# Moving TensorE's broadcast of B behind the y sums and products of its step

## The reference, cut to what matters

```python
dA = jnp.exp(jnp.einsum('ble,en->blen', delta, A))
dBu = jnp.einsum('ble,bln,ble->blen', delta, Bm, u)
def step(h, inp):
    dA_t, dBu_t, C_t = inp
    h = dA_t * h + dBu_t
    y_t = jnp.einsum('ben,bn->be', h, C_t)
    return (h, y_t)
```

## Time and profile before

| | |
|---|---|
| median of 3 runs | 494.55 us (493.66 to 495.66) |
| the profiled execution's own time | 495.33 us |
| its span | 493.5 us |
| busy: PE / DVE / ACT / POOL | 406.7 / 447.3 / 378.1 / 422.7 us |
| idle of PE just before the broadcast | 37.7 us |
| idle of DVE just before `dbu` | 3.7 us |
| mean granted clock of PE | 0.94 |

### The profile page before, as it was taken

How to read it: one execution, slowest core, us unless ns; L and a number is a source line. 1 busy time by engine, 2 the same in 40 slices (tenths; PEclk the granted TensorE clock), 3 DMA queues, 4 the chain that set the end, 5 groups by cost and what they waited for, 6 DMA issues and landing times. The chain is left out here.

```text
span 493.5 us, 6708 instructions
## 1 busy us (share of the span) xinstructions
PE 406.7 (82%) x2133; PEld 279.7 (57%) x2164; DVE 447.3 (91%) x539; ACT 378.1 (77%) x690; POOL 422.7 (86%) x236
## 2 busy tenths in 40 slices
PE   7969665997499698997799788996899697687796
PEld 3537444675358456674558556664658455565474
DVE  6698899979999899989999889988999889999852
ACT  4478975598867898698967898698966898687715
POOL 6159899999999789998999899988999789999810
PEclk9999987997889989998999999998999989599799
DMA  6673045200830028300742027300741027300001
GB/s 168 160 298 151 1 144 222 87 0 1 301 126 27 0 42 327 108 0 2 248 149 77 2 66 303 106 2 0 259 156 60 1 62 306 107 2 21 0 1 43
DMA packets 24146, 51.06 MB, mean 103 GB/s; under 512 B 4521, under 2 KB 14256, under 8 KB 20016
## 3 DMA queue, kind: packets, MB, share of 16 engines
q1 hardware_dynamic: 24112, 50.64, 30.1%
HBM read 48.01 MB, written 2.62 MB: 103 GB/s over the span
## 5 line engine op out<-in xcount | busy, mean ns | idle before, releaser
L606 POOL TENSOR_TENSOR hc<-h,c_rows 128x1024 f32<-128x1024 f32 x127 | 298.4, 2366 | 27.0 <-DVE h L1382 26.3
L1382 DVE TENSOR_TENSOR_SCAN h<-dA,state,dbu 128x512 f32<-128x512 f32 x192 | 234.2, 1266 | 13.2 <-ACT dA L697 13.2
L697 ACT ACTIVATE dA<-delta,a_neg 128x512 f32<-128x512 f32 x256 | 173.2, 685 | 45.3 <-DVE h L1382 44.9
L1123 PE MATMUL yb<-ident,hc 128*128 128x128 f32 x1024 | 155.1, 287 | 17.8 <-POOL hc L606 16.6
L1123 PEld LDWEIGHTS yb<-ident,hc 128*128 128x128 f32 x1024 | 131.0, 149 | 64.9 <-issue 45.0
L1395 DVE TENSOR_TENSOR dbu<-du,bb 128x1024 f32<-128x1024 f32 x88 | 105.5, 1199 | 3.7 <-PE bb L1148 2.0
L593 POOL TENSOR_TENSOR dbu<-du,b_rows 128x1024 f32<-128x1024 f32 x40 | 94.6, 2364 | 4.1 <-DMA b_rows<-bc_dram 4.1
L1382 DVE TENSOR_TENSOR_SCAN h<-dA,dbu 128x512 f32<-128x512 f32 x64 | 74.2, 1205 | 5.5 <-ACT dA L697 5.4
L1023 PE MATMUL mf<-f_hT,w_conv 128*128 128x512 f32 x112 | 54.6, 612 | 2.0 <-ACT zu L757 1.4
L1148 PE MATMUL bb<-b_parts,sel 128*128 128x512 bf16 x63 | 25.1, 399 | 37.7 <-DVE dbu L1395 36.4
L1148 PEld LDWEIGHTS bb<-b_parts,sel 128*128 128x128 bf16 x88 | 8.6, 98 | 56.5 <-DVE dbu L1395 36.9
(11 more groups left out here) (206 smaller groups left out, 524.2 us busy)
## 6 DMA issues: line engine op xcount, KB each, us to landing
c_rows<-bc_dram SPq DMA_DIRECT2D x32, 1024.0 KB, 7.5
b_rows<-bc_dram SPq DMA_DIRECT2D x40, 256.0 KB, 8.9
xs<-in_L_attn_x_dram SPq DMA_DIRECT2D x8, 256.0 KB, 3.6
out_dram<-xs SPq DMA_DIRECT2D x7, 256.0 KB, 5.6
ygT<-in_L_attn_conv_w_dram SPq DMA_DIRECT2D x2, 256.0 KB, 4.3
bc_dram<-xd SPq DMA_DIRECT2D x8, 64.0 KB, 1.6
w_in<-in_L_attn_W_in_dram SPq DMA_DIRECT2D x2, 128.0 KB, 4.2
probT<-in_L_wmod_dram SPq DMA_DIRECT2D x1, 256.0 KB, 4.2
```

The lines of the kernel that those rows point to most:

```text
L606: nc.gpsimd.tensor_tensor(hc[:, pair % RC, :, :], h[:, pair % RH, :, :], c_rows[:, q, n % NQ, :].unsqueeze(1).broadcast_to([P, HALVES, T]) ...
L697: nc.scalar.activation(dA[ke % RD][:, :], delta[:, ge % 2, half, :], ACT.Exp, scale=a_neg[:, half, n:n + 1]).then_inc(s_dA, 1)
L1123: last = nc.tensor.matmul(bank[:, tile], hc[:, pair % RC, half, tile], ident[:, :], start=False, stop=n == N - 1, is_transpose=True, skip_ ...
L1382: v.tensor_tensor_scan(h[:, pair % RH, half, :], dA[k % RD][:, :], dbu[:, pair % RW, half, :], start, ALU.mult, ALU.add).then_inc(s_scan, 1)
```

## The change

The block that makes the broadcast moves from the head of PE's step to behind the y sum, the products of both sides and the correction product of B. Its condition, its waits and its instruction stay as they are, and no other engine's list changes.

```diff
                 for s in range(STEPS):
                     k = g * STEPS + s
                     kf, ks = k + AHEAD_FILL, k - LAG_SUM
-                    if 0 <= kf < K and kf % HALVES == 0 and kf // HALVES % N not in POOL_N:
-                        pair = kf // HALVES
...
-                        nc.tensor.matmul(bb[mine % RB][:, :], sel[:, n, :], b_parts[:, gf % 2, :],
-                                         start=True, stop=True).then_inc(s_fill, 1)
                     if 0 <= ks < K:
                         y_sum(ks)
                     for side in JOBS:
...
                                         skip_group_check=True).then_inc(s_r1 if s == F_R1 else s_r2, 1)
+                    if 0 <= kf < K and kf % HALVES == 0 and kf // HALVES % N not in POOL_N:
+                        pair = kf // HALVES
+                        gf, n = divmod(pair, N)
+                        if n == 0:
+                            pe.wait_ge(s_lo, gf + 1)
+                        if pair == 0:
+                            pe.wait_ge(s_wdtc, 1)
+                            pe.wait_ge(s_sel, 1)
+                        mine = by_dve(pair)
+                        if mine >= RB:
+                            pe.wait_ge(s_dbu, mine - RB + 1)
+                        nc.tensor.matmul(bb[mine % RB][:, :], sel[:, n, :], b_parts[:, gf % 2, :],
+                                         start=True, stop=True).then_inc(s_fill, 1)
                     if g == 0 and s in W_TURN:
```

## The result

The changed kernel takes 509.16 us (median of 4 runs, 508.53 to 509.39) against 495.00 us (4 runs, 493.66 to 495.66): ratio 1.0297, 95% interval 1.0275 to 1.0319. It is slower by 14.2 us; 509.4 was forecast. The profiled execution took 509.13 us, with a span of 507.3, 13.8 more than before.

What follows compares the result with a forecast made beforehand. DVE's sequence sets the time, so each late broadcast adds one to one. Terms 0.5 + 1.1 + 3.9 + 8.9 + 0.4 = 14.8 us on the profiled 495.33, less 0.8 for the median, gave 509.4 us; range 503 to 516.

Steps and rivals of the forecast that it cites:

- Step 21: Groups 2 to 6: broadcast behind a leaf sum that waits for ACT's read of `probT`; 1.78 us late, 8.9 in all.
- Step 3: Groups 2 to 6: broadcast lands late behind half of a u product; 0.4 to 1.0 us each, 3.9 in all.
- Step 11: Broadcast 1.5 us late, but swallowed by DVE's existing 1.53 us wait for an exponential straight after; no cost.
- Steps 5 and 23: Broadcast late too, but covered: earlier delays at steps 3 and 21 exceed the 0.1 to 1.1 us lost; no cost.
- Step 9: Broadcast late, but covered by earlier delays larger than the 0.1 to 1.1 us it loses; no cost.
- Group 1: Delay of 2.2 us at step 3, of which ACT's slack at step 10 takes 1.1; net 1.1 us.
- Group 0: First `dbu` 0.6 us late, some 2.3 at step 3, less 1.21 and 0.9 absorbed; net 0.5 us, bounds 0 and 1.3.
- The end: Last broadcast, step 27 of group 7, moves behind a leaf sum where PE sets the end; 0.4 us, bounds 0.2 and 1.1.
- The rival on the clock: Less PE idle time lets the last leaf sums run at 2.4 GHz, 3.45 us of work in 1.7: 507.7 us; 3%.
- The 36.4 us frees nothing: PE's idle time in front of the broadcast gets partly filled by y sums, freeing nothing that DVE waits for.
- Half of it is absorbed: Rival: of step 21's delay and the next group's at steps 3 and 9, only the larger counts; 503 to 506 us; 16%.
- The covers fail: Rival: steps 11 and 9 add 0.5 to 1.5 us in several groups, ACT's silu block delayed too; 515 to 520 us; 14%.

Runs made afterwards that it cites:

- e1: Kernel before, with the broadcast moved behind the y sum and leaf sum in step 21 only: 503.85 us, ratio 1.0196.
- e6: Changed kernel, with the broadcast back in front in step 3 only: 506.08 us, ratio 1.0237 against the kernel before.
- e4: Kernel before, with the broadcast moved behind in step 11 only: 494.47 us, ratio 0.9996.
- e2: Kernel before, with the broadcast moved behind in step 23 only: 501.76 us, ratio 1.0142.
- e3: Kernel before, with the broadcast moved behind in steps 21 and 23 only: 505.36 us, ratio 1.0225.
- e5: Changed kernel, with the broadcast back in front in step 21 only: 508.40 us, ratio 1.0289 against the kernel before.
- e12: Kernel before, unchanged, run again for a third profile: 495.01 us.
- e7: Kernel before, with the broadcast moved behind only in steps 15, 17, 27, 29 and 31: 497.40 us, ratio 1.0053.
- e8: Kernel before, with the broadcast moved behind the y sum but in front of the products, in all steps: 495.58 us, ratio 1.0028.
- e9: Kernel before, with the broadcasts of steps 3, 5, 9 and 11 moved one step earlier: 501.14 us, ratio 1.0135.

## Why the prediction was right

**The bound and the method** held. DVE's busy time stayed (447.3 to 448.9), and every delay of the broadcast beyond two scans was paid one to one, except ahead of a wait that DVE had anyway: at step 13, at step 9 of group 1, and for 0.48 us at step 28 of group 4, where the prediction saw no slack.

**Step 21** was the best term: five times 1.78 was worked out from the earlier trace rows, 1.62 to 1.99 came, and e1 has it alone. The key was to see that the leaf sum waits for `probT`, a read by ACT, and that this wait would now stand in front of the broadcast.

**Step 3** was 0.6 us too small over five groups (3.9, came 4.5). The mis-sized place is group 2: 0.4 taken, 0.66 came, which is 0.97 at step 3 less 0.31 up to step 13. I had granted it that PE would get there sooner; group 4 has 1.08 (taken 1.0), groups 3, 5 and 6 0.98, 1.07 and 0.70 (0.94, 0.94, 0.66). e6 confirms it from the other side, by its scans: what groups 2 to 6 add falls from 12.9 to 8.4 us. (Its time falls only by 3.1, because of groups 0 and 1.)

**Step 11** is covered as said: e4 is some 9 us of exchanged waiting at no cost, and 1.53 became 0.24 (near 0.3 forecast).

**Steps 5 and 23** are covered as said. **Step 9** costs nothing for another reason than was said. Step 3's delay does not cover it: it adds 0.13 to 0.36 us in groups 2 to 6, and the same in e6, where step 3 has no delay; the wait ahead of step 13 takes it back. The cover of 23 is a property of the whole change, not of the step: e2 gives step 23 a price of 6 us alone, e3 none behind step 21, and e5 shows it charged as soon as step 21's delay is away. The prediction gave 5, 9 and 23 "0.1 to 1.1 us that the broadcast loses", which fits the 0.98 to 1.17 of four groups in e2; the fifth has 1.47.

**Group 1** was too large: 1.1 forecast, 0.3 came. The delay at step 3 was 1.4, not 2.2. The prediction took PE's place in step 3 from the earlier trace rows as the kernel's own, but the clock of one execution had made it. Here is half a u product of step 0, three steps ahead, in the profile of before:

```profile
84.19 3.50 PE L1023 MATMUL mf<-f_hT,w_conv 128*128 128x512 f32 x4
```

And the same in the changed kernel's profile, where PE then waits for `hc` in step 3:

```profile
85.26 1.88 PE L1023 MATMUL mf<-f_hT,w_conv 128*128 128x512 f32 x4
...
91.07 0.66 PE L1123 MATMUL yb<-ident,hc 128*128 128x128 f32 x4 [1.33 <-POOL hc L606]
```

The granted clock was 0.57 from 84 to 88 us before and 1.00 from 85 to 89 after. So PE comes to step 3's product 0.8 us sooner against DVE than was reckoned. In e12, the unchanged kernel with less of the low clock there (2.51 us for that half), DVE's wait of 0.54 at this place is gone too. Of the 1.4 us, 0.69 went at the `dbu` that reads step 9's broadcast, for which DVE had waited 0.83 before (the forecast had not used this), and 0.43 at step 13.

**Group 0** came near: 0.6 for 0.5, with a first wait of 0.81 where 0.6 was said. This is luck in part. The terms that the prediction gives for it (0.6, 2.3, less 1.21 and 0.9) come to 0.8, not 0.5. And the unchanged kernel alone adds 2.5 us in group 0 and takes off 0.9 in group 1 between its first profile and e12's, so no single profile can tell such small terms. Ahead of it stand 1.1 us by which the profiled execution got to its first `dbu` later. The start of the scans differs by 0.8 us or more among the experiments, in both directions, so I do not count that to the change.

**The end**: 0.7 us at the last broadcast for 0.4 forecast, and -1.9 that the forecast did not have. e12 shows this second part in the unchanged kernel. The rival on the clock priced just this (3.45 us of work in 1.7) but tied it to the change; it is where the clock falls in one execution. The start's +1.1 and the end's -1.9 nearly cancel, so the match to 0.3 us is partly luck; the other terms sum to 14.5. Among them 1.4 us too much (group 1 and the rest of groups 2 to 6) stand against 1.1 too little (step 3, the last broadcast and 0.1 twice). One reading of the prediction stands on a row that isn't there: the earlier trace rows don't show PE idle ahead of the slow stretch. The row before them in the trace does, 0.66 us busy of 2.00:

```profile
461.00:463.00 2.00, 0.66 (x4) 0.42 (x4) 2.00 (x3) 1.99 (x3) 2.00 (x2) 0.97 0.00 0
```

**"The 36.4 us frees nothing"** was right for this change and too broad as a sentence. e7 and e8 give PE's idle time back in part and gain nothing. But e9 shows that the idle time is free only up to the length it has: with 10 us more of it the kernel takes 6.2 more.

**The rivals.** "Half of it is absorbed" needed steps 3 and 21 to hide each other; both are in the account, and hiding reaches two steps (21 to 23), not the 14 to the next group's step 3. "The covers fail" is refuted by e4 and e3. "Faster" needed products that end before the second scan; the earlier trace rows excluded it, and so do the 23 waits for `bb`. "Nothing" is refuted by the time, and by e1's 18.3 us for `dA`, 0.4 less than before. The range of 503 to 516 was said to take in most of the first two rivals; of the second (515 to 520) it takes in only the edge.

**What it said one would see**: some 18 us of waits for `bb` with at least ten entries; there are 25.6 with 23. The difference is step 11's: its seven exchanged waits, 7.2 us here, were priced right and left out of this sentence.

## What to carry to other kernels

When one buffer ties an in-order engine to the one that sets the time, give each instruction of the tie a deadline (buffer free, buffer needed) and look at what stands in front of it. A wait of the engine that has slack is no loss, and filling it is no gain; but a wait on a third engine put in front of the tie is paid in full, every time, and so is the tie put so far forward that the work behind it becomes late. Price edits as a set: of the same two steps one costs 9 us, the other 6, both together 9, and undoing only the larger gave back 0.8 (some 3 by the estimate without e5's slow stretch).

## What the runs showed of the hardware that was not expected

Where TensorE's clock falls to half differs between executions of one kernel. The unchanged kernel had a granted clock of 0.50 from 463 to 467 us in one profile and 1.00 in another, and the stretch behind the last scan differs by 1.97 us. From 30 to 38 us it is the other way round, 1.00 in the first profile and 0.57 in e12, and group 0 is 2.46 us longer there. The spans differ by 0.3. Nothing in PE's list was different. The Trainium skill says in "TensorE: Matmul & The Clock Gate", Part 1, that the same kernel differs from run to run by the phase of the gate at its start, and that the penalty of this ramp is under 1% of a typical span. The traces agree in size (2.5 us are 0.5% of 494) and show the difference at the end of the kernel as well. The Trainium skill's section "Why this matters for your kernels" on the same page advises to keep TensorE busy continuously, to get the full clock. No run here does that. The nearest is e8, whose y sums run in part of the idle time (PE waits 25.4 us for `dbu` in front of the broadcast, against 42.0): it is 1.1 us slower, and its granted clock is 0.944 in the mean of its ten runs, against 0.950 in the 16 of the kernel before.

For the reader of profiles it means that a difference of up to 2.5 us in one stretch of PE-bound work, even where it repeats in one pair of profiles, is to be checked against a second profile of the same kernel before a cause is given to it.
